# Four graph layers on one core: products of tile pairs in the edge loop, and row terms placed ahead of the network's last activations

## The reference

```python
x = _layernorm(x + gat(x, edge_index))            # 8 attention heads of 64 features, softmax over the edges of a node
x = _layernorm(x + equivariant(x, edge_attr_4, edge_attr_8, edge_index))
x = _layernorm(x + kan(x, edge_index))            # attention over neighbours, then splines
x = _layernorm(x + neighbour_mean(x, edge_index))
```

```python
h = edge_feats                                    # 8 features an edge
for W in (W_mlp1, W_mlp2, W_mlp3):
    h = SILU_2MOM * silu(h @ W / sqrt(W.shape[0]))    # the network: 64 hidden features
w1, w2, w3, w4 = split(h @ W_mlp4 / 8.0, 4)       # four weights of 128 an edge
s0, s1 = x0[sender], x1[sender]                   # 128 scalars and 3 x 128 vector parts
p1 = w1 * s0 * y0
p2 = (w2 * s0)[:, :, None] * y1[:, None, :]
p3 = w3[:, :, None] * s1 * y0[:, None, :]
p4 = w4 * einsum('eum,em->eu', s1, y1) / sqrt(3)
msg = segment_sum of (p1, p4) and (p2, p3) over the receiver
```

## Time and profile before

| | |
|---|---|
| median of three runs | 1622.65 us |
| profiled execution | 1622.43 us |
| its span, first to last instruction | 1620.6 us |
| mean granted TensorE clock | 0.957 |
| busy: TensorE, VectorE, ScalarE, GpSimd | 1413.8, 1325.7, 748.8, 490.5 us |
| edge loop, first product to last sum | 698.3 to 1028.1 us |
| attention heads, first to last tile | 407.5 to 636 us |
| packets of the two instruction queues | 33 and 28 |

### The profile page before, as it was taken

How to read it: one execution, slowest core, us unless ns; L and a number is a source line. 1 busy time by engine, 2 the same in 40 slices (tenths; PEclk the granted TensorE clock), 3 DMA queues, 4 the chain that set the end, 5 groups by cost and what they waited for, 6 DMA issues and landing times.

```text
span 1620.6 us, 24360 instructions
## 1 busy us (share of the span) xinstructions
PE 1413.8 (87%) x7887; PEld 791.9 (49%) x7887; DVE 1325.7 (82%) x2088; ACT 748.8 (46%) x1591; POOL 490.5 (30%) x489
## 2 busy tenths in 40 slices
PE   1978999528787888699999999969999999999997
PEld 1555545303333334666666666855544444444465
DVE  8885999997999999679999999789567747874144
ACT  1285665428555655645555555533144523331400
POOL 1788888740000111066666666000000000000000
PEclk9998999759899999789999999979999999999999
DMA  4201000126102210366666667100211120121301
GB/s 135 58 6 8 6 7 6 38 70 176 64 32 62 63 36 20 112 185 194 196 195 191 188 192 180 33 1 26 99 54 54 52 78 26 52 99 40 125 26 45
DMA packets 70906, 130.91 MB, mean 81 GB/s; under 512 B 12890, under 2 KB 31436, under 8 KB 70717
## 3 DMA queue, kind: packets, MB, share of 16 engines
q0 software_dynamic: 23568, 60.29, 14.8%
q1 hardware_dynamic: 44531, 63.26, 11.8%
q10 hardware_dynamic: 2746, 6.59, 1.2%
HBM read 106.43 MB, written 23.47 MB: 80 GB/s over the span
## 4 chain that ended last, share of the span: by engine, by line
PE 37%; DVE 22%; issue 17%; POOL 15%; DVEq 4%; DMA 3%; ACT 2%; POOLq 0%; ACTq 0%
PE PS L1249 19%; POOL recs L681 15%; DVE arena L1984 7%; PE PS L1214 5%; DVE arena L2141 4%; DVE arena L1980 3%; PE PS L1331 3%; PE PS L1311 2%; DVE arena L2133 2%; DVEq L2151 1%; PE PS L1321 1%; DVEq L2141 1%; DVE arena L2132 1%; PE PS L1176 1%; DVE cnt_d L1765 1%
## 5 line engine op out<-in xcount | busy, mean ns | idle before, releaser
L1249 PE MATMUL PS<-arena 128*125 128x512 f32 x640 | 275.2, 592 | 0.0
L681 POOL DMA_INDIRECT recs<-arena x170 | 247.0, 1453 | 89.6 <-issue 89.3
L1619 ACT ACTIVATE arena<-arena,gslot 128x32 f32<-128x32 f32 x832 | 182.0, 307 | 144.8 <-DVE arena L2124 140.6
L746 POOL DMA_INDIRECT arena<-xup,gidx x208 | 197.5, 950 | 117.4 <-issue 50.6
L1037 PE MATMUL PS<-arena 125*128 125x512 f32 (+1 forms) x480 | 190.8, 536 | 43.8 <-DVE arena L1984 43.8
L1125 PE MATMUL PS<-arena 128*32 128x128 f32 (+1 forms) x3328 | 218.8, 305 | 7.3 <-ACT arena L1619 2.0
L1125 PEld LDWEIGHTS PS<-arena 128*32 128x32 f32 x3328 | 169.5, 109 | 107.6 <-ACT arena L1619 55.2
L2133 DVE TENSOR_TENSOR arena<-PS,arena 128x768 f32<-128x768 f32 x208 | 200.1, 962 | 0.0
L1249 PEld LDWEIGHTS PS<-arena 128*125 128x125 f32 x640 | 120.0, 188 | 154.1 <-issue 153.6
L1037 PEld LDWEIGHTS PS<-arena 125*128 125x128 f32 x480 | 86.3, 192 | 148.2 <-issue 78.4
L1564 ACT ACTIVATE arena<-arena,c 125x1250 f32<-125x1250 f32 x80 | 106.8, 1337 | 101.2 <-DVE arena L1980 101.2
(11 more groups left out here) (376 smaller groups left out, 2150.8 us busy)
## 6 DMA issues: line engine op xcount, KB each, us to landing
arena<-in_spline_wT SPq DMA_DIRECT2D x16, 1024.0 KB, 5.2
arena<-uv_rows SPq DMA_DIRECT2D x14, 610.4 KB
arena<-h_rows SPq DMA_DIRECT2D x26, 256.0 KB, 4.4
h_rows<-arena SPq DMA_DIRECT2D x24, 256.0 KB, 2.8
arena<-xup,gidx POOLq DMA_INDIRECT x208, 3.5
cnt_rows<-cnt_s SPq DMA_DIRECT2D x1, 3051.8 KB
recs<-arena POOLq DMA_INDIRECT x170
xup<-arena SPq DMA_DIRECT2D x10, 250.0 KB
```

Of the source, the lines that this page charges most:

```text
L681: pool.indirect_dma_start(out=recs, out_offset=bass.IndirectOffsetOnAxis(pos[:, c:c + 1], 0), in_=rec[:, c, :], in_offset=None).then_inc(s ...
L746: pool.indirect_dma_start(out=ring[:, m, :], out_offset=None, in_=xup, in_offset=bass.IndirectOffsetOnAxis(gidx[:, par, m:m + 1], 0))\
L1249: return t.matmul(PS[:NP, y2_bank(half, b), :], lhs[:, (k * HB + b) * NP:(k * HB + b + 1) * NP], w[:, k * D:(k + 1) * D], start=(first and ...
L1619: ins = A(sel4[:, s, y * DB:(y + 1) * DB], eq4[:, m // 4, s * DB:(s + 1) * DB], ACT.Copy, scale=gslot[:, par, c + R_Y + y:c + R_Y + y + 1])
```

## The change

In the edge loop VectorE's products are made for a pair of tiles at once, in two instructions of 512 and 1536 columns in place of four. The order becomes: scalar products of pair j + 1, sum of tile 2j - 1, vector products of pair j + 1, sum of tile 2j. The comparison stays on VectorE, ahead of the scalar products of every second pair. The loop is written out for all 208 tiles on VectorE; the other engines keep theirs. The scalar products wait for both gathers and both weights of the pair; the signal to TensorE and GpSimd comes once for both tiles.

At the handover, the row terms are made as transposes, the first half after the last but one `layer3`, the second half after it and ahead of the last `layer3`; ScalarE copies the halves ahead of its last two `silu3`. These two write to a buffer of their own, `hid3_end`, which lies under nothing of the first tiles. VectorE no longer waits for `s_mlp_done` but, ahead of its second tile, for the stores of `hid3`; ScalarE waits for the stores of `hid3_end` at block 3 of head 0. The copies of head features move behind the first and the fourth exponential. `s_mlp_done` is given right behind the last `silu3`.

```diff
+        hid3_end = at(13000, [128, 4, GS // 2])
@@ TensorE, the network
+                if m == NM - 1:
+                    pe.wait_ge(s_uv_ok, 1)
+                    row_products(0, 0)
+                    pe.wait_ge(s_hid_ok, silu_no[2, NM - 1])
+                    row_products(1, H)
             pe.wait_ge(s_uv2_in, 6)
+            pe.wait_ge(s_hid_ok, silu_no[3, NM - 1])
             uv_transposes(uv, 2 * H, s_uvt_ps, 5)
@@ TensorE, row_products
-                    ins = t.matmul(PS[:NP, 3 * q + b // 4, (b % 4) * NP:(b % 4 + 1) * NP],
-                                   uv[:, b, col:col + 1].to_broadcast([NP, NP]), ident[:NP, :NP], start=True, stop=True)
+                    ins = t.transpose(PS[:NP, 3 * q + b // 4, (b % 4) * NP:(b % 4 + 1) * NP],
+                                      uv[:, b, col:col + 1].to_broadcast([NP, NP]), ident[:NP, :NP])
@@ ScalarE, the network
-                if m >= 2:
+                if 2 <= m < NM - 2:
                     act.wait_ge(s_h3_out[s], 16 * (m // 2))
                     act.wait_ge(s_h3_out[s + 1], 16 * (m // 2))
+                if m >= NM - 1:
+                    rows_in(UV[:, 0, :, :], m - (NM - 1), 0)
                 if m >= 1:
                     silu3(m - 1)
...
+            act.sem_inc(s_mlp_done, 1)
             A(expw[:], epsc[0:1, 0:1], ACT.Exp, scale=0.0)
-            rows_in(UV[:, 0, :, :], 0)
-            for q in range(4):
-                act.wait_ge(s_h3_out[q], 16 * (NCH // 4))
-            act.sem_inc(s_mlp_done, 2)
@@ ScalarE, a head
                     if sblk == 0 and before is None:
+                        first_features(0)
                         evac_uv(uvrow_sb, 2 * H, 5, s_uvrow_ok, s_uvt_ps)
+                    if sblk == 3 and before is None:
+                        first_features(1)
+                        act.wait_ge(s_h3_end, 64)
@@ VectorE, the first head
             dve.wait_ge(s_uv2_in, 6)
-            dve.wait_ge(s_mlp_done, 1)
...
             for sblk in range(LEAD):
+                if sblk == 1:
+                    for q in range(4):
+                        dve.wait_ge(s_h3_out[q], 16 * (NM - 2) // 2)
                 first_step(0, 0, 0, sblk)
@@ VectorE, the edge loop
+            def scalar_products(j):
+                m, par = 2 * j % TP, j // 4 % 2
+                xg, w, pr = of_pair(j)
+                if j % 4 == 0:
+                    dve.wait_ge(s_gidx_ok, j // 4 + 1)
+                if j % 2 == 0:
+                    dve.wait_ge(s_sel_ok, 2 * j + (2 * TP - 4))
...
+                dve.wait_ge(s_gath[m], 16 * (j // 4 + 1))
+                dve.wait_ge(s_gath[m + 1], 16 * (j // 4 + 1))
+                dve.wait_ge(s_tpw_ps, 2 * j + 2)
+                v.tensor_tensor(pr[:, :, :, 0, :], w[:, :, :, 0, :], xg[:, :, 0:1, :].to_broadcast([128, 2, 2, MUL]), ALU.mult)
+
+            def vector_products(j):
+                xg, w, pr = of_pair(j)
+                v.tensor_tensor(pr[:, :, :, 1:4, :], w[:, :, :, 1, :].unsqueeze(3).to_broadcast([128, 2, 2, 3, MUL]),
+                                xg[:, :, 1:4, :].unsqueeze(2).to_broadcast([128, 2, 2, 3, MUL]), ALU.mult).then_inc(s_prod_ok, 2)
...
-            with dve.Fori(0, G // 4 - 1) as i:
-                two_groups(i, 0)
-                two_groups(i, 1)
...
+            for j in range(NT // 2):
+                if j + 1 < NT // 2:
+                    scalar_products(j + 1)
+                if j >= 1:
+                    add_sums(2 * j - 1, 2 * j - 1, words[(2 * j - 1) // 4])
+                if j + 1 < NT // 2:
+                    vector_products(j + 1)
+                if j % 2 == 0:
+                    words.append(dve.value_load(gpk[0:1, j % 4 // 2, j // 4:j // 4 + 1], min_val=0, max_val=64 ** 4 - 1))
+                add_sums(2 * j, 2 * j, words[j // 2])
+            add_sums(NT - 1, NT - 1, words[-1])
```

More of the change, by code:

```diff
@@ L463, in build @@
         NCH = -(-NDG // DGB) * 4
+        assert NDG % DGB == DGB // 2
         def width(blk):
@@ L986, in layer3, with row_products @@
                                  start=True, stop=True, tile_position=(r, o)).then_inc(s_mlp_ps, 1)
+            def row_products(q, col):
+                for b in range(NB):
+                    ins = t.transpose(PS[:NP, 3 * q + b // 4, (b % 4) * NP:(b % 4 + 1) * NP],
+                                      uv[:, b, col:col + 1].to_broadcast([NP, NP]), ident[:NP, :NP])
+                    if b % 4 == 3 or b == NB - 1:
+                        ins.then_inc(s_uvt2_ps, 1)
             feat_transposes(0)
@@ L2114, in _, with of_pair @@
             dve.sem_inc(s_gsum_ok, 4)
[L2116 to L2122 removed]
+            def of_pair(j):
+                m, s = 2 * j % TP, 2 * j % 4
+                xg = ring[:, m:m + 2, :].rearrange("p t (q n) -> p t q n", q=4)
+                w = PS[:, (0, 6)[j % 2]:(0, 6)[j % 2] + 2, :].rearrange("p t (h g n) -> p t h g n", h=2, g=2)
+                return xg, w, prod[:, s:s + 2, :].rearrange("p t (h q n) -> p t h q n", h=2, q=4)
@@ L2141, in add_sums @@
                 v.tensor_tensor(d, PS[:, 2 + m % 4, 0:256], d, ALU.add).then_inc(s_gsum_ok, 1)
[L2143 to L2160 removed]
+            scalar_products(0)
+            vector_products(0)
+            words = []
+            for j in range(NT // 2):
[9 more added lines that the diff above has]
+            add_sums(NT - 1, NT - 1, words[-1])
             dve.wait_ge(s_gsum_ok, NT + 4)
```

63 lines of the change are left out of this document (15 added, 48 removed).

## The result

| | before | after |
|---|---|---|
| median of 6 runs each | 1624.77 us | 1608.05 us |
| lowest to highest | 1617.5 to 1634.87 | 1607.27 to 1610.74 |
| ratio, 95% interval | | 0.9899, 0.9873 to 0.9925 |
| profiled execution, its span | 1620.6 | 1605.7 |
| first head tile (VectorE) | 407.50 | 401.48 |

The account below looks back on a forecast made before the run. VectorE was taken to pace the edge loop at 3.155 us a pair, TensorE 2% behind and the next bound; 1622.4 less 9.1 (loop) and 4.8 (handover) gave 1608.5 us, range 1602.5 to 1619.5.

Parts of the forecast that it names:

- The price of VectorE's products: Edge loop: merged products at 1.025 ns a column plus 0.07 us fixed take 0.60 and 1.65 us.
- the slow pattern: Rival, edge loop: merged instruction a tenth below the column rate, 3.22 us a pair, 1625.3 us; chance 0.10 including no gain.
- The order of the sums: Edge loop: scalar products between two sums make the step 0.93 us, hiding the 0.78 wait with 0.15 to spare.
- Unrolling: Edge loop on VectorE: register work shrinks but runs beside VectorE's instructions either way, worth nothing.
- One-hots: Edge loop: scaled one-hots come before their tile's products, so TensorE's 0.2 us wait put down to ScalarE goes.
- Start and end: Edge loop's ends: start loses 1.1 us waiting for two gathers, end loses 0.15 us by a later last scatter.
- Handover: Edge network to attention heads: VectorE's first head tile starts at 402.7 against 407.50, 4.8 us won.
- It becomes the bound: Edge loop: TensorE, needing 3.05 us a pair, becomes the bound, so the gain is 0.105 a pair.
- the first rival: Edge loop: VectorE stays the bound, gaining 0.145 us a pair, 13.1 us in the loop, 1604.5 us; chance 0.12.
- The loop over latencies: Edge loop: the round trip between TensorE and VectorE over two periods takes 6.04 to 6.22 us, 3.02 to 3.11 a pair.
- the rival of a lock: Edge loop: TensorE and VectorE hold each other at 3.11 us a pair, 1614.4 to 1618.9 us; chance 0.20.
- code loading: Rival, written-out edge loop: instruction loads wait behind gathers, losing 35 to 71 us, 1643 to 1680 us; chance 0.06.

Follow-up runs that it names:

- sums_together: Changed kernel with both sums of a step ahead of the vector products, one behind the other; 1662.66 us, ratio 1.0234.
- third_of_vectors: Changed kernel with only the first of three vector components multiplied on VectorE; 1596.03 us, ratio 0.9831.
- two_comparisons: Changed kernel with VectorE's one-hot comparison made for the first eight tiles only, later tiles reusing those; 1606.63 us, ratio 0.9896.
- rows_by_products: Changed kernel with the handover's row terms made as products again instead of transposes, in the new order; 1610.24 us, ratio 0.9916.
- unroll_only: Kernel before with VectorE's single-tile edge loop written out for all 208 tiles, nothing merged; 1622.98 us, ratio 0.9989.
- late_terms_after: Changed kernel with about 3.1 us of extra VectorE reductions ahead of the row terms' inputs; 1611.94 us, ratio 0.992.
- late_terms_before: Kernel before with about 3.1 us of extra VectorE reductions ahead of the row terms' inputs; 1625.15 us, ratio 1.0008.
- loop_only: Kernel before with the new edge loop and the old handover; 1611.1 us, ratio 0.9917.

## Why the prediction came out, and which step failed

**Right, and measured as such.**

- *The price of VectorE's products.* 1.025 ns a column and 0.07 fixed gave 0.60 and 1.65; the rows show 0.60 and 1.66. The longer access pattern costs nothing that can be seen, so the slow pattern falls. The saving is the 0.07 for each instruction merged away. The 120 fixed cycles of the Trainium skill ("VectorE: DVE Perf Modes", errata of TRN2) would have given 26 us in the loop; the steady part gave 11.56. Between instructions that follow without a wait, the trace doesn't agree with that figure.
- *The order of the sums.* 0.93 between two sums hides the 0.78; sums_together shows the price if it doesn't, 0.53 a pair.
- *Unrolling* at nothing: 0.4 at most. The Trainium skill ("Runtime: NRT & Kernel Launch", instruction fetch mechanics) lets a taken branch cost a stall only where its target lies outside the two blocks of 256 instructions that are held. A turn of VectorE's old loop has about 160 instructions in the trace, so by that section no stall was due, against what the prediction drew from it. The trace agrees with it: VectorE is busy 40.00 of 40 in the earlier trace rows, and 40.00 with the loop written out.
- *One-hots* in time: ready 1.7 us or more before the scatter in after. The sign named for it, the wait on ScalarE gone from the list, did not come, since that wait was never one for ScalarE.
- *Start and end*: 1.26 for 1.1 in the profiled execution (1.0 to 2.9 over all), 0.18 for 0.15.
- *Handover*: 4.8 for 4.8 in the profiled execution, with the transposes at 1.22 a half; the waits for stores hidden.

**The step that failed: "It becomes the bound, so the gain is 3.155 - 3.05 = 0.105, not 0.145."** TensorE's need was read off a pair that shows no wait in its row, and was 0.10 too high: third_of_vectors has 2.946 in the mean. VectorE stayed the bound, the mechanism of the first rival, which had been given 0.12. That the total still came out is an accident of sizes: VectorE gained 3.154 - 3.033 = 0.121 a pair and not the 0.145 of its bare instructions. Of the 0.024 between, 0.016 is the four-tile period of the timeline, 6.05 for 6.02 in the sum (vector products 1.66 for 1.65, and rounding of starts). The other 0.007 a pair, 0.7 us in all, stands in five of the 48 periods, of 6.07 to 6.37; one holds a gap of 0.23 put down to issue, the rest is not traced further. The loop so gave 10.1, between the forecast's 9.1 and the rival's 13.1.

Of the signs that the prediction named, two came out against it: VectorE's idle time ahead of the scalar products is not there, and the wait put down to ScalarE's one-hots stayed in the list (44.7). The prediction took that label at its word, also for the 0.2 us in the second pair of the earlier trace rows. In before too the scatter of a pair's second tile starts 0.13 or less behind that tile's products, with its one-hots ready for 0.9 us or more: TensorE was waiting for VectorE's products in both kernels. It has 3.033 - 2.946 = 0.09 a pair to spare.

**The loop over latencies** was the prediction's better instrument, with two terms off. It has 1.99 for the scatters (1.89 in two_comparisons) and 0.06 for the signal from VectorE to TensorE (0.13). With them it closes at 3.005 a pair and not at 3.02 to 3.11. That is 0.02 under VectorE's 3.026, so the rival of a lock fell by little: a VectorE faster by more than that would have met it, and not TensorE's own need.

**Not foreseen:** TensorE's new wait for VectorE's terms. The prediction took every half from the layer-3 product on and never asked when the terms were ready; in the trace of before they end at 394.4, 4.1 us ahead of the 398.5 where the prediction's first half begins, but in other executions the network ends up to 5.5 us earlier and the terms don't. Of the seven executions with the new order and the terms left alone, TensorE waits for them in five, and in three of these (sums_together, two_comparisons, rows_by_products; granted 0.50, 0.57 and 0.62 from 396 to 400) its clock falls. There the new order, with transposes, is worth about half of the 4.8, as far as the one execution of the old order with the clock down tells. That the 4.8 came in full in after is luck of that execution, whose network ended late (395.59).

**The rest.** The slower rivals fell: no lock (after's VectorE doesn't idle), no code loading (no gap in the 48 periods is over 0.23). The chances had 0.69 on faster by over 0.5%, which came.

## What to carry to other kernels

A pair without a wait in its row is not yet an engine's need: where another engine sets the pace, its hold can sit inside a merged row. Cut the work of the pacing engine in an experiment, read what the follower does then, and only then say what becomes the bound. The next bound need not be an engine at all: here it is the way round from TensorE to VectorE and back, 3.005 a pair, which a large cut (third_of_vectors) steps over and a small one (two_comparisons) runs into. The name that a profile gives for a wait is a guess: compare the start of what waited with the ends of all that it needs. Merging instructions that follow one another without waits is worth the fixed step between starts (here 0.07 us each), while the distance between dependent instructions is worth far more, so place something between them first. When a step is moved ahead, ask of each of its inputs when it is ready, and not only of the one it used to stand behind.

## What the runs showed of the hardware

- The granted clock of TensorE stood at 0.50, the lower of its levels (1.2 GHz), behind idle waits of 1.99 (unroll_only), 2.44 (sums_together) and 4.51 us (late_terms_after), and at 1.00 behind waits of 1.32, 1.66, 2.21 (late_terms_before) and 2.58 (loop_only). So the length of the wait alone doesn't say whether the clock falls. Where it fell, twenty transposes took 4.56 in place of 2.44: a short wait ahead of a short block can cost as much by the clock as by itself.
- Twenty fp32 transposes against an identity are 20 records and 2.44 us; the same as products are 40 records and 4.63.
- From the end of VectorE's products to the start of TensorE's loads that wait for them it took 0.13 to 0.15 us, from the end of TensorE's product to VectorE's instruction that waits for it 0.17 to 0.18 (after, two_comparisons, third_of_vectors).
- A sum on VectorE that waits for the sum just before it starts 0.78 us behind it, one that follows without a wait 0.33.
